# Graph layers on one Trainium2 core: GpSimd's gathers wait for a nearer product

## The chip, the core and the metric

The kernel runs on one core of one Trainium2 chip. The metric is device time in microseconds (us) from start to end of one execution; of several executions the median counts. The engines are TensorE (PE in the profile; its weight loads are PEld), VectorE (DVE), ScalarE (ACT), GpSimd (POOL) and SyncE (SP). They have a queue of instructions each and meet by semaphores.

## What is computed

Four residual blocks on 6250 nodes with 256 features, joined by 106,250 directed edges sorted by target: a graph block, a feed-forward block with 8 experts, a second graph block, a second feed-forward block with 8 experts. Each graph block holds two graph convolutions, so there are four edge sums, called layers 0 to 3 here. The reference, cut to the edge sums:

```python
# first graph block (layers 0 and 1)
deg_out = segment_sum(edge_weight, src); deg_in = segment_sum(edge_weight, dst)
norm = edge_weight * rsqrt(deg_out[src] * deg_in[dst] + EPS)
h6 = relu(segment_sum((h5 @ W6)[src] * norm[:, None], dst) + b6)
h7 = relu(segment_sum((h6 @ W7)[src] * norm[:, None], dst) + b7)
out = h7 @ Wp + bp
# second graph block (layers 2 and 3): the norm comes from target degrees alone
m = (h @ W)[src] * norm[:, None]
x1 = segment_sum(m, dst) + b
...
x = x + gnn0(layernorm(x)); x = x + ffn0(layernorm(x))
x = x + gnn1(layernorm(x)); x = x + ffn1(layernorm(x))
```

## The kernel before

**Tiling.** The edges lie in chunks of 128, and four chunks (`Q`) make a group: 208 groups (`NGR`) in layers 0 and 1. In layers 2 and 3 part of the edge sum is done as products with tables of counts, and 116 groups (`NGK`) are left. The nodes are 49 tiles (`NT`) of 128 rows. For each group GpSimd fetches the rows of the source nodes from a table in HBM, four indirect DMAs (line 915) of 128 rows of about 1 KB, each to the partitions of one chunk. TensorE multiplies these rows by a selection matrix of the group, four chunk products summed in PSUM (line 1091); the product has the sums of the group's edges by target node. VectorE adds it to `ACC`, the sums of all nodes (line 2102).

**The ring of rows.** The gathered rows go to `RS_` = 8 slots of one group each, in layer 0 up to group 37 also to 11 further slots in a tile that is needed for something else later; in layers 2 and 3 a ring of `RK` = 4 slots is used. `gather_edges` is GpSimd's loop over the groups. Ahead of a group's four gathers it waits on the semaphore `s_p`, which counts the products of TensorE, until the product of the group that held the slot before is done: the group eight back in the middle of layers 0 and 1, four back in layers 2 and 3. The first groups of a layer find free slots. `BEGIN` = (0, 208, 416, 532) holds the count of products at a layer's start.

**TensorE**, `sum_edges` (from line 1259): for each group it waits for the group's rows (`wait_rows`, one semaphore per slot, line 1265) and for its scaled selection matrix, makes the product and counts it in `s_p`. In between stand pieces of other work as soon as a tile of nodes has its sums: its transposes (`early_turn`, line 1129), the next layer's dense products (lines 1134 and 1136 in layer 0), and in layers 2 and 3 the products with the counts (lines 1219 and 1239).

**VectorE**, in layer 0 `sum_weighted`, per group g and in this order:

```python
multiply_degrees(g + 3)   # line 2276: waits until the rows of group g+3 have landed
invert(g + 2)             # line 2282, after a square root on ScalarE (line 1562)
...                       # selection for group g+4 (line 2066)
weigh(g + 2)              # line 2286; ScalarE then scales the selection (line 1569)
...                       # degrees and places of group g+4 (lines 2091, 2075)
ve.wait_ge(s_p, g + 1)
step(add_sums(g % 4, spot))   # line 2102, two instructions
```

The out-degree of a source node comes with its row, which is why the weights of layer 0 need the rows. In layers 1 to 3 VectorE makes the selections and the adds, and touches no gathered row; ScalarE scales the selection of layer 1 (line 1639).

The order on each engine is the order of the code; no scheduler moves it.

Of the kernel before, what the change touches and what calls it, by code (L numbers as in the profile page):

```python
# [20 lines left out]
RS_ = 8  # L21
# [4 lines left out]
NC = -(-(-(-NE // P)) // 16) * 16  # L26
NGR = NC // Q
AHEAD = 4
BEHIND = 5
UP, DOWN = 2, 4  # L30
W = 64
# [31 lines left out]
RK = 4  # L63
# [3 lines left out]
BEGIN = (0, NGR, 2 * NGR, 2 * NGR + NGK)  # L67
# [3 lines left out]
def ready_groups(pace, groups):  # L71
    done = [max(0, ((g - pace[1]) * pace[0]) >> 10) for g in range(groups)]
    return [min([g for g in range(groups) if done[g] > t], default=groups) for t in range(NT)]


READY = [ready_groups(pace, groups) for pace, groups in zip(PACE, GROUPS_OF)]
TAIL = min(t for t in range(NT) if READY[0][t] + AHEAD >= NGR)
EARLY = [{READY[layer][t] + AHEAD: t for t in range(TAIL)} for layer in range(3)]
assert all(g + 4 < NGR for g in EARLY[0] if EARLY[0][g] < TAIL - 1)
assert all(g + DOWN < NGR and g + UP + 1 < NGR for g in EARLY[1] if EARLY[1][g] < TAIL - 1)  # L80
assert NT - TAIL == 3 and all(len(early) == TAIL for early in EARLY)
assert all(READY[layer][TAIL - 1] + AHEAD + 2 == GROUPS_OF[layer] for layer in range(3))
KV = Q + 1
# [54 lines left out]
def gnn_ffn(nc, x, src, dst, edge_weight, W6, b6, W7, b7, Wp, bp, Wr, br, W1a, b1a, W2a, b2a, gamma, beta,  # L138
# [23 lines left out]
    with ctx:  # L162
# [3 lines left out]
        def sem(name):  # L166
            return ctx.enter_context(nc.semaphore(name))
# [116 lines left out]
        NS = len(SEL)  # L284
        assert NS > AHEAD
        META = WORK[:, 3 * U * D:3 * U * D + 2 * EC]
# [153 lines left out]
        s_p, s_pe = sem("sums_ready"), sem("sums_more")  # L440
# [49 lines left out]
        def in_x(layer, g):  # L490

            return layer == 0 and g < 2 * ROUND and g % ROUND >= RS_

        def turn_of(layer, g):

            n = BEGIN[layer] + g
            return n % ROUND + n // ROUND * RS_ if n < 2 * ROUND else n - 2 * PX

        def group_of_turn(m):

            return m % RS_ + m // RS_ * ROUND if m < 2 * RS_ else m + 2 * PX
# [3 lines left out]
        def late_turn(layer, g):  # L505
            return divmod(BEGIN[layer] - BEGIN[2] + g, RK)

        def slot_of(layer, g):
            if layer >= 2:
                return late_turn(layer, g)[1]  # L510
            return g % ROUND - RS_ if in_x(layer, g) else turn_of(layer, g) % RS_

        def rows_of(layer, g):
            if layer >= 2:
                return LATE_ROWS[slot_of(layer, g) * Q:(slot_of(layer, g) + 1) * Q]
            return (ROWS_X if in_x(layer, g) else ROWS)[slot_of(layer, g) * Q:(slot_of(layer, g) + 1) * Q]
# [362 lines left out]
        def _(po):  # L879
# [18 lines left out]
            def gather_edges(layer, tab, width):  # L898
                for g in range(GROUPS_OF[layer]):
                    m = turn_of(layer, g)  # L900
                    if layer == 2 and g < RK:
                        po.wait_ge(s_free, 4 + BEGIN[2])
                    elif layer >= 2:
                        po.wait_ge(s_p, BEGIN[layer] + g - RK + 1)
                    elif in_x(layer, g):
                        if g >= ROUND:
                            po.wait_ge(s_p, g - ROUND + 1)
                    elif m >= RS_:
                        po.wait_ge(s_p, group_of_turn(m - RS_) + 1)
                    if layer == 0 and 2 <= g < ROUND:  # L910
                        po.wait_ge(s_dp, RS_ * (g - 1))
                    landed = (s_rx if in_x(layer, g) else s_row)[slot_of(layer, g)]
                    for k, rows in enumerate(rows_of(layer, g)):
                        c = Q * g + k
                        po.indirect_dma_start(  # L915
                            out=rows[:, 0:width], out_offset=None, in_=tab[:, :],
                            in_offset=bass.IndirectOffsetOnAxis(ap=SRC[:, c:c + 1].bitcast(u32), axis=0))\
                            .then_inc(landed, 16)
# [39 lines left out]
            po.wait_ge(s_dost, 16)  # L958
            po.wait_ge(s_span, 1)
            gather_edges(0, tab1, ROW1)  # L960
            gather_wide(tab1, ROW1)

            table_stored(TAB2)
            po.wait_ge(s_sums, 1)
            gather_edges(1, tab2, D)
            gather_wide(tab2, D)
            po.sem_inc(s_wi, 1)

            table_stored(TAB3)
            gather_edges(2, tab3, D)  # L970
            gather_wide(tab3, D)
            table_stored(TAB4)
# [18 lines left out]
            def tokens(n):  # L991
                rows = min(P, CAP - n % RB * P)
                col = n // RB % 2 * RB + n % RB
                return rows, bass.IndirectOffsetOnAxis(ap=IDB[0:rows, col:col + 1].bitcast(u32), axis=0)

            po.wait_ge(s_by, 16 * NI)
            po.wait_ge(s_out, 16 * (NI + 1))
            for n in range(E1 * RB + BEHIND):
                if n < E1 * RB:
                    rows, which = tokens(n)  # L1000
                    po.wait_ge(s_idb, n // RB + 1)
                    if n >= U:
                        po.wait_ge(s_sum, n - U + 1)
                    po.indirect_dma_start(out=XIN[0:rows, n % U * D:(n % U + 1) * D], out_offset=None,
                                          in_=before_y[:, :], in_offset=which).then_inc(s_xg[n % U], 16)
                if n >= BEHIND:
                    m = n - BEHIND
                    rows, which = tokens(m)
# [841 lines left out]
        def _(ve):  # L1850
# [191 lines left out]
            def load_window(g):  # L2042
                if g % RS_ == 0:
                    firsts[g // RS_] = first_nodes(g)
# [10 lines left out]
            def edges(v, g):  # L2055
                return v[:, bass.ds(Q * g, Q)]
# [7 lines left out]
            def select(into, places):  # L2064

                return ve.tensor_tensor(  # L2066
                    by_window(into), PLACES[:, 0:W].rearrange("p (a n) -> p a n", a=1).to_broadcast([P, Q, W]),
                    by_edge(places).to_broadcast([P, Q, W]), ALU.is_equal)
# [15 lines left out]
            def number_places():  # L2084

                step(ve.tensor_copy(PLACES, IOTA[:, :]))
                settle()
# [200 lines left out]
            def sum_weighted():  # L2288

                number_places()  # L2290
                for g in range(AHEAD):
                    load_window(g)
                    load_spots(g)
                    step(place(SEL[g], edges(DST, g)))
                ve.wait_ge(s_sz, 1 + len(SPREADS))
                for g in range(AHEAD):
                    step(select(SELD, edges(REL, g)))
# [1068 lines left out]
```

## Time and profile before

| | us |
|---|---|
| median of 3 runs | 5292.09 (5290.26 to 5301.05) |
| profiled execution, first to last instruction | 5305.9 |
| TensorE busy | 3977.3 (75%) |
| VectorE busy | 2919.9 (55%) |
| GpSimd busy | 2859.7 (54%) |
| GpSimd's gathers of edge rows (line 915) into the ring, 2504 | 2411.9 |
| layer 0, first to last gather | 240.4 to 1533.8 |
| layer 1 | 1558.9 to 2856.3 |
| layer 2 | 3271.8 to 3990.2 |
| layer 3 | 4013.7 to 4707.3 |

The profiled execution's own time is its span; with the profiler it lies 13.8 us above the median. Before layer 0 stand the first normalisation, the first dense product and the degrees; between layers 1 and 2 the first feed-forward block; after layer 3 the second. Busy times are averages over these stages, and no engine is full: in the four edge sums what matters is who waits for whom. A row of the timeline tells an instruction's start, its duration, engine and line, and in brackets how long its engine stood idle before it and what ended that; "remote" is a wait whose end fits no instruction just finished.

### The profile page before, as it was taken

To read this page: it belongs to the slowest core of one execution; us is meant where nothing else is said; L and a number is where in the kernel's file an instruction comes from. 1 tells how busy PE (TensorE), PEld (TensorE's weight loads), DVE (VectorE), ACT (ScalarE), POOL (GpSimd) and SP (SyncE) were. 2 spreads that over 40 slices of the span, in tenths; PEclk is the share of its full clock that TensorE was granted. 3 is DMA by queue.
4 is the path that set the end of the run, shared out by engine and by line. 5 is a ranking of instruction groups with operands and counts; after the bars stand their busy time and mean duration, and the time that the engine had idled before them with its cause. 6 is when DMAs were issued, how large, how long until landed. Compare 5 with 4: busy or idle time off the path is not lost.

```text
span 5305.9 us, 64097 instructions
## 1 busy us (share of the span) xinstructions
PE 3977.3 (75%) x20960; PEld 3151.6 (59%) x20961; DVE 2919.9 (55%) x7680; ACT 1417.2 (27%) x3894; POOL 2859.7 (54%) x3104
## 2 busy tenths in 40 slices
PE   6775655454555576777777996899996898886999
PEld 6653434343434455666666665787785777764666
DVE  7755655455546775555656556776665332243344
ACT  6603323232331222222222331333331000033221
POOL 7745566666656665565653002566565666643322
PEclk9857776777777777777777998999998999997999
DMA  3332343333333232222322002444444554444321
GB/s 92 106 70 78 110 112 100 98 99 99 97 95 90 86 87 79 81 85 81 86 81 66 25 14 74 130 144 144 138 146 140 160 155 138 138 136 135 103 80 54
DMA packets 337524, 535.23 MB, mean 101 GB/s; under 512 B 91587, under 2 KB 246452, under 8 KB 337186
## 3 DMA queue, kind: packets, MB, share of 16 engines
q0 software_dynamic: 133168, 361.15, 24.1%
q1 hardware_dynamic: 196902, 163.10, 10.0%
q10 hardware_dynamic: 7118, 6.83, 0.4%
q8 instruction: 171, 2.80, 0.2%
q14 instruction: 165, 1.35, 0.1%
HBM read 439.58 MB, written 94.26 MB: 101 GB/s over the span
## 4 chain that ended last, share of the span: by engine, by line
PE 54%; DVE 19%; issue 11%; another core or an unknown queue 11%; ACT 2%; DVEq 1%; POOL 1%; DMA 0%; ACTq 0%; SPq 0%; POOLq 0%
PE PSA L1091 15%; PE PSA L1239 12%; PE PSA L1486 4%; PE PSA L1472 4%; PE PSA L1248 4%; DVE ACC L2102 3%; PE PSA L1373 3%; PE PSA L1389 3%; DVE XIN L2075 2%; DVE XT L2075 2%; PE PSA L1041 1%; PE PSA L1219 1%; ACT ACC L1536 1%; DVE PSA L2066 1%
## 5 line engine op out<-in xcount | busy, mean ns | idle before, releaser
L915 POOL DMA_INDIRECT WORK<-tab,SRC x2504 | 2411.9, 963 | 1923.8 <-issue 666.6
L2102 DVE TENSOR_TENSOR ACC<-ACC,PSA 64x256 f32 x1296 | 541.9, 418 | 1221.2 <-remote 686.6
L1091 PE MATMUL PSA<-WORK,XIN 128*128 128x256 f32 x3032 | 881.2, 443 | 362.7 <-ACT XIN L1569 156.8
L1091 PEld LDWEIGHTS PSA<-WORK,XIN 128*128 128x128 f32 x3032 | 653.7, 225 | 490.5 <-issue 387.9
L1091 PE MATMUL PSA<-WORK,XT 128*128 128x256 f32 x1976 | 581.2, 446 | 217.8 <-ACT XT L1569 131.9
L1091 PEld LDWEIGHTS PSA<-WORK,XT 128*128 128x128 f32 x1976 | 427.7, 226 | 302.6 <-issue 226.4
L1239 PE MATMUL PSA<-WORK 128*128 128x256 bf16 x2730 | 367.0, 278 | 16.7 <-issue 16.5
L1239 PEld LDWEIGHTS PSA<-WORK 128*128 128x128 bf16 x2730 | 270.1, 100 | 60.7 <-issue 24.7
L2075 DVE TENSOR_TENSOR XIN<-PSA,DST 128x512 f32<-128x512 f32 x392 | 265.3, 679 | 3.9 <-issue 1.9
L1729 ACT ACTIVATE WORK<-PSA 128x512 bf16<-128x512 f32 x245 | 146.4, 598 | 428.1 <-PE PSA L1219 328.4
L1639 ACT ACTIVATE XIN<-XIN,HSB 128x128 f32<-128x128 f32 x504 | 160.2, 392 | 359.7 <-DVE XIN L2075 231.5
L1248 PE MATMUL PSA<-WORK 128*128 128x50 f32 x832 | 133.6, 313 | 133.1 <-DVE XT L2075 84.8
L1486 PE MATMUL PSA<-ACC,WORK 128*128 128x256 f32 (+1 forms) x1024 | 230.3, 379 | 0.0
L1248 PEld LDWEIGHTS PSA<-WORK 128*128 128x128 f32 x832 | 127.1, 230 | 151.1 <-DVE XT L2075 94.5
L1472 PE MATMUL PSA<-WORK,ACC 128*128 128x489 f32 (+1 forms) x512 | 213.4, 577 | 0.4 <-ACT WORK L1834 0.4
L1248 PE MATMUL PSA<-WORK,XT 128*128 128x50 f32 x832 | 132.5, 312 | 105.5 <-issue 55.6
L1486 PEld LDWEIGHTS PSA<-ACC,WORK 128*128 128x128 f32 (+1 forms) x1024 | 185.7, 185 | 31.4 <-issue 3.5
L1248 PEld LDWEIGHTS PSA<-WORK,XT 128*128 128x128 f32 x832 | 129.1, 231 | 120.9 <-issue 60.6
L954 POOL TENSOR_SCALAR ACC<-IOTA,ACC,HSB 128x64 f32<-128x64 int16 x312 | 177.0, 582 | 36.3 <-PE PSA L1041 19.7
L1041 PE MATMUL PSA<-ACC 128*64 128x98 f32 x1664 | 163.3, 252 | 44.2 <-ACT ACC L1536 43.2
L1802 ACT ACTIVATE WORK<-PSA 128x256 f32<-128x256 f32 x51 | 19.6, 385 | 651.4 <-remote 331.3
L2771 DVE TENSOR_TENSOR WORK<-WORK,PSA 128x10 f32 x208 | 33.6, 162 | 277.0 <-remote 166.0
(511 smaller groups left out, 6768.4 us busy)
## 6 DMA issues: line engine op xcount, KB each, us to landing
WORK<-tab,SRC POOLq DMA_INDIRECT x2504
unit_counts_d<-WORK SPq DMA_DIRECT2D x245, 128.0 KB
WAX<-unit_counts_d SPq DMA_DIRECT2D x140, 128.0 KB
ACC<-in_L_ffn_w SPq DMA_DIRECT2D x16, 1024.0 KB
WORK<-unit_counts_d SPq DMA_DIRECT2D x105, 128.0 KB
tab<-WORK SPq DMA_DIRECT2D x98, 128.0 KB
slots_x<-FILL SPq DMA_DIRECT2D x4, 2080.0 KB
ACC<-slots_x SPq DMA_DIRECT2D x8, 910.0 KB
```

Of the source, the lines that this page charges most:

```text
L915: po.indirect_dma_start(out=rows[:, 0:width], out_offset=None, in_=tab[:, :], in_offset=bass.IndirectOffsetOnAxis(ap=SRC[:, c:c + 1].bitca ...
L954: last = po.tensor_scalar(LOWW[:, k * LOW:(k + 1) * LOW], IOTA[:, 0:LOW], S_LO[:, c:c + 1], EW[:, c:c + 1], ALU.is_equal, ALU.mult)
L1041: last = pe.matmul(hsrc, LOWW[:, k * LOW:(k + 1) * LOW], HI[:, k * HIGH:(k + 1) * HIGH], start=(b == 0 and j == 0), stop=(b == NBT - 1 and ...
L1091: last = pe.matmul(PS[h][:, 0:D], chosen[:, j * P:(j + 1) * P], rows[:, 0:D], start=(j == 0), stop=(j == Q - 1))
L1239: last = pe.matmul(UNS[i][t % 2], UNC[i][n % len(UNC[i])][:, part * P:(part + 1) * P], part_of(2 * u + h, c), start=(u == 0 and h == 0 and ...
L1248: last = pe.matmul(MOVES, TO[k % 2][:, j * P:(j + 1) * P], MOVED[k // Q % 2][:, c * 2 * KX:(c + 1) * 2 * KX], start=(j == 0), stop=(j == Q ...
L1373: last = pe.matmul(PS[q % 4][:, 0:GT // 2], W1S[:, w:w + P], XT0[:, c * GT + hf * (GT // 2):c * GT + (hf + 1) * (GT // 2)], start=(c == 0) ...
L1472: last = pe.matmul(PS[q % 4][:, 0:hn], W1L[:, w:w + P], XT1[:, c * CAP + h0:c * CAP + h0 + hn], start=(c == 0), stop=(c == KC - 1))
L1486: last = pe.matmul(PS[BK + r % BK][0:rows, 0:D], H1[:, f * CAP + r * P:f * CAP + r * P + rows], W2L[:, (k * FC1 + f) * D:(k * FC1 + f + 1) ...
L1639: last = ac.activation(part, part, ACT.Copy, scale=NRM[:, Q * g + j:Q * g + j + 1])
L2075: return ve.tensor_tensor(by_place(into), PLACES.rearrange("p (a n) -> p a n", a=1).to_broadcast([P, Q, P]), by_edge(places).to_broadcast( ...
L2102: return ve.tensor_tensor(rows, rows, PS[h][half, 0:D], ALU.add)
```

## The change

A second wait ahead of a group's gathers, on the same semaphore. In layer 0 from group 60 on, group g waits until the product of group g-4 is counted; in layer 1 from group 8 on, and in layers 2 and 3 from group 4 on, until that of group g-3 is. The old waits stay; except where the slots of the layer's first groups are free, they are met when the new one is. No instruction of an engine is added, taken away or moved besides: the 572 waits (148, 200, 112 and 112) stand on GpSimd's queue, each ahead of the first of a group's four gathers. In the changed file the lines behind the two additions are three further down (915 becomes 918).

```diff
 AHEAD = 4
+NEAR = (4, 3, 3, 3)
 BEHIND = 5
...
                     if layer == 0 and 2 <= g < ROUND:
                         po.wait_ge(s_dp, RS_ * (g - 1))
+                    if g >= (60, RS_, RK, RK)[layer]:
+                        po.wait_ge(s_p, BEGIN[layer] + g - NEAR[layer] + 1)
                     landed = (s_rx if in_x(layer, g) else s_row)[slot_of(layer, g)]
                     for k, rows in enumerate(rows_of(layer, g)):
```

## Rows read from the trace of the kernel before

**Rows 1.** The page: the chain that ended last, shares of the span by engine.
```profile
PE 54%; DVE 19%; issue 11%; another core or an unknown queue 11%; ACT 2%; DVEq 1%; POOL 1%; DMA 0%; ACTq 0%; SPq 0%; POOLq 0%
```
**Rows 2.** Windows, layers 0-3: length, busy us of PE, PEld, DVE, ACT, POOL; clock, DMA, GB/s.
```profile
680.00:1534.00 854.00, 450.79 (x1475) 333.52 (x1474) 448.08 (x1336) 257.75 (x814) 562.79 (x594) 0.72 0.36 98
...
1621.00:2857.00 1236.00, 874.57 (x3989) 749.58 (x3990) 773.95 (x1867) 288.88 (x926) 770.60 (x788) 0.78 0.29 84
3309.00:3990.00 681.00, 624.33 (x4515) 529.20 (x4516) 468.83 (x1113) 225.87 (x507) 417.83 (x436) 0.98 0.47 140
4060.00:4707.00 647.00, 578.43 (x4048) 478.61 (x4046) 203.30 (x456) 18.88 (x49) 410.25 (x431) 0.96 0.50 146
```
**Rows 3.** Lines of 680 to 1534: count, busy us, mean ns, idle before by cause.
```profile
L915 POOL DMA_INDIRECT WORK<-tab,SRC x594 | 562.8, 947 | 291.3 <-issue 170.2 <-remote 104.9 <-PE PSA L1091 16.1
```
**Rows 4.** Waits of 680 to 1534: us in total, times, longest us.
```profile
POOL WORK L915 <- remote: 104.9, 31, 4.0
```
**Rows 5.** Timeline, one burst of layer 0: start, us, engine, line [idle before].
```profile
1012.63 0.95 POOL L915 DMA_INDIRECT WORK<-tab,SRC  x1 [3.90 <-remote]
...
1013.84 0.23 DVE L2276 TENSOR_TENSOR PRD<-DIE,WORK 128x4 f32<-128x4 f32 x1
...
1016.15 3.75 PE L1091 MATMUL PSA<-WORK,XIN 128*128 128x256 f32 x8 [6.05 <-ACT XIN L1569]
...
1021.42 1.89 PE L1091 MATMUL PSA<-WORK,XT 128*128 128x256 f32 x8
...
1026.37 1.97 PE L1091 MATMUL PSA<-WORK,XIN 128*128 128x256 f32 x8 [1.11 <-ACT XIN L1569]
...
1035.50 0.85 DVE L2102 TENSOR_TENSOR ACC<-ACC,PSA 64x256 f32 x2 [9.62 <-remote]
1035.63 0.95 POOL L915 DMA_INDIRECT WORK<-tab,SRC  x1 [3.27 <-remote]
```
**Rows 6.** Timeline, layer 0 while GpSimd issues nothing: two of nine adds, then GpSimd.
```profile
574.71 0.85 DVE L2102 TENSOR_TENSOR ACC<-ACC,PSA 64x256 f32 x2 [3.80 <-PE PSA L1091]
...
601.33 0.85 DVE L2102 TENSOR_TENSOR ACC<-ACC,PSA 64x256 f32 x2
604.02 0.95 POOL L915 DMA_INDIRECT WORK<-tab,SRC  x1 [31.95 <-PE PSA L1091]
```
**Rows 7.** Timeline of GpSimd in the last stage.
```profile
4757.80 0.97 POOL L986 DMA_INDIRECT slots_x<-WORK,IDS  x1 [0.30 <-issue]
```
**Rows 8.** Timeline, the ends of layers 0 and 1: gathers and last adds.
```profile
1532.84 0.95 POOL L915 DMA_INDIRECT WORK<-tab,SRC  x1 [0.30 <-issue]
...
1549.08 0.85 DVE L2102 TENSOR_TENSOR ACC<-ACC,PSA 64x256 f32 x2 [1.10 <-PE PSA L1091]
...
2851.05 0.94 POOL L915 DMA_INDIRECT WORK<-tab,SRC  x1 [2.06 <-PE PSA L1091]
...
2880.01 0.85 DVE L2102 TENSOR_TENSOR ACC<-ACC,PSA 64x256 f32 x2 [2.31 <-PE PSA L1091]
```
**Rows 9.** Timeline, the start of layer 1.
```profile
1558.89 0.95 POOL L915 DMA_INDIRECT WORK<-tab,SRC  x1 [25.10 <-SPq L696]
...
1572.66 0.95 POOL L915 DMA_INDIRECT WORK<-tab,SRC  x1 [0.30 <-issue]
1573.38 0.85 DVE L2102 TENSOR_TENSOR ACC<-ACC,PSA 64x256 f32 x2 [17.93 <-issue]
...
1575.45 1.99 PE L1091 MATMUL PSA<-WORK,XIN 128*128 128x256 f32 x8 [0.56 <-DMA WORK<-tab,SRC]
...
1620.96 0.95 POOL L915 DMA_INDIRECT WORK<-tab,SRC  x1 [5.28 <-remote]
```
**Rows 10.** Timeline, GpSimd in layer 2: first and last gather of one group, then the next.
```profile
3455.05 0.95 POOL L915 DMA_INDIRECT WORK<-tab,SRC  x1 [1.39 <-PE PSA L1091]
...
3458.90 0.95 POOL L915 DMA_INDIRECT WORK<-tab,SRC  x1 [0.30 <-issue]
...
3461.07 0.95 POOL L915 DMA_INDIRECT WORK<-tab,SRC  x1 [1.22 <-PE PSA L1091]
```

## The prediction

> **What bounds the kernel now.** I read the chain of waits first, to learn where the end is decided, then the busy time by stage, then single bursts in the timeline. The chain [rows 1] gives TensorE 54% and VectorE 19%, but also 11% to "another core or an unknown queue", on a kernel with one core: the engine waited for a signal whose sender had, by its own rows, finished long before. Those stretches lie in the four edge-sum stages, so I read these by themselves. In the windows [rows 2] one group (four gathers) takes 854/148.5 = 5.75 us in layer 0, 1236/197 = 6.27 in layer 1, 681/109 = 6.25 in layer 2 and 647/107.75 = 6.00 in layer 3. GpSimd needs 0.947 us for a gather and 0.30 us to the next, 5.0 us per group. In layer 0 that is almost all there is: of the 854 us, 562.8 are busy, 170.2 are those 0.30 us steps, and only 104.9 + 16.1 us are waits for products [rows 3], 31 of them labelled remote [rows 4], 3.4 us each. Layer 0 is bound by GpSimd plus one pause of 3.4 us per four or five groups. In layers 1 to 3 GpSimd's four gathers cost 5.0 us of 6.0 to 6.3, so it waits after every one to three groups: the ring is full and each gather is let go by a product. There the summing side is the bound.
>
> How the two sides meet is in the timeline of layer 0 [rows 5]. GpSimd starts at 1012.63 and issues 16 gathers without a stop, to 1032.36. The product at 1021.42 ends by its row at 1023.31, the third one after it starts at 1026.37 and ends at 1028.34, yet VectorE gets the first of these signals only for its add at 1035.50, after 9.62 us idle, and GpSimd resumes at 1035.63, 3.27 us after its own last gather. While GpSimd is idle, from 572.07 to 604.02, nothing like it occurs: nine adds from 574.71 to 601.33, 3.33 us per group [rows 6]. So while gathers are issued without a break, TensorE's signals can come late, and a pause of GpSimd lets them through.
>
> *The Trainium skill's page "Perfetto Trace Analysis", section "Tensor Engine Instruction (MATMUL, LD_WEIGHTS)", says that a matmul's end in a trace is estimated from its size, and that its signal goes out only when PSUM has acknowledged the data. By it the product may in truth have ended late, and the row at 1021.42 alone can't refute that; the idle stretch [rows 6] speaks for GpSimd as the cause either way.*
>
> **The change part by part.** No instruction moves on any engine. A group's first gather waits in addition for a nearer product: four back in layer 0 from group 60 on, three back elsewhere, where it was eight back (layers 0 and 1) or four back (layers 2 and 3). Queued behind that wait on GpSimd are only the following gathers; who then waits for these is VectorE in layer 0 (line 2276 needs the rows of group g+3 before the add of group g) and TensorE in layers 1 to 3. There are 148 + 200 + 112 + 112 = 572 such waits.
>
> 1. *The waits themselves.* Every one is a further wait ahead of a gather that has one already. The nearest row is the gather at 4757.80 in the last stage: its code has two waits too, both met, and its distance to the one before is the usual 0.30 us [rows 7]. So I take 0; the row's last digit allows 0.02 us, 572 x 0.02 = 11 us at most.
>
> 2. *Layer 0, the switch at group 60.* GpSimd must wait there for a product that lies four groups later. At 3.33 us per group with GpSimd idle [rows 6] that is 13.3 us in place of one ordinary pause of 3.4: its queue is 10 us later. At the layer's end it gets some back: now the last gather ends at 1533.79 and the last add at 1549.93, 16.1 us later [rows 8]. With four groups left, the last rows must land, 1.84 us (a gather ends at 1573.61 and the product that waits for it starts at 1575.45 [rows 9]), and pass multiply, weights and product. I take 12 us, between 8.8 (landing, the 6.1 us chain of step 3, one add of 0.85) and the 16.1 of today: 4 us back. Sum +6, bounds -4 (if the summing side, not GpSimd's queue, sets the end) and +10.
>
> 3. *Layer 0, steady.* After a pause three products are signalled together, so three groups may go, 15.0 us. The fourth needs the next product. Its weights come after VectorE's multiply for the first group gathered since the pause: that lands at 4.7 + 1.84 = 6.6 us. From a multiply at 1013.84 to the end of the product that it leads to, 1016.15 + 3.75 = 1019.90, it is 6.1 us [rows 5]. So the permission comes at 12.7 us, 2.3 us before it is wanted, bursts stay at four, and the term is 0. Without that slack bursts get shorter: two groups cost (10.0 + 2.06)/2 = 6.03 us per group (2.06 is the pause after two groups at 2851.05 [rows 8]), so +0.28 x 148 = +41 us; one group 5.0 + 1.3 = 6.3 [rows 10], +81 us; three lie near +20 us, an estimate between zero and 41.
>
> 4. *Layer 1, the switch at group 8.* Now GpSimd issues eleven groups in one go to 1615.68 and resumes at 1620.96, and from the first add at 1573.38 on only four adds fall into that time [rows 9]. With the change it stops after eight, 1558.89 + 8 x 5.0 = 1599. From there I give four groups 3.33 us each: six adds by 1612 instead of four by 1621, that is 9 + 2 x 6.27 = 21 us ahead. At the end the last eight groups take 2880.01 - 2851.05 = 29 us, 3.6 each [rows 8], because no gather runs beside most of them; with three left, five of them go at 6.27, +13 us. Sum -8, bounds -21 and +13.
>
> 5. *Layers 1 to 3, steady.* GpSimd is let go by products before and after: in layer 2 it starts at 3455.05, its last gather starts at 3458.90, the next group starts at 3461.07 behind a product's signal after 1.22 us [rows 10]. The same signal lets go a group that is nearer by one (layers 2, 3) or five (layer 1); GpSimd's starts don't move. The rows must then be there in time: a group lands 4.7 + 1.84 = 6.6 us after the signal, and three groups at 6.0 to 6.3 us leave 18 us. Term 0; the one group of difference at start and end of layers 2 and 3 is (6.25 - 3.33) = 2.9 us won and about the same lost, +-3 each.
>
> Sum: +6 + 0 - 8 + 0 + 0 = -2 us. The profiled execution has a span of 5305.9 us, 13.8 above the median of 5292.09; the terms are differences and I put them on the median: 5290 us. The outer bounds of the five terms, without a change of burst length, give -31 to +40; all extremes together are unlikely, and half of it, 5276 to 5312, holds most of this case.
>
> **The rivals.** *Slower: layer 0 loses its lead.* VectorE takes its work in order, and the multiply of group g+3 stands ahead of the add of group g. Four deep, every landing lies just ahead of that multiply: the 2.3 us of slack in step 3 is hardly more than the difference between a product that takes 3.75 us and one that takes 1.89 [rows 5]. It decides from the point at which the product four back comes later than 15 us into a burst. Bursts of two to three groups give +20 to +41, 5310 to 5333.
>
> *The Trainium skill's "DMA: Bandwidth & Descriptors", section "Rules for kernel authors", advises to issue a DMA early and to wait for it late, so that its fixed cost lies beside other work. The change issues 572 groups later than the ring allows; by that rule it ends on this rival's side. The rows bear that out for layer 0 only, where the slack is small; in layers 1 to 3 step 5 shows 18 us to cover 6.6.*
>
> *Faster: less run-ahead, shorter stalls.* If the late signals [rows 5] come from long unbroken bursts, a GpSimd that runs out of permissions sooner lets them through sooner. For it speaks the start of layer 1 [rows 9], where the burst of eleven groups stops the adds; against it that in the steady stages the ring is full and permissions are used as they come, so that the bursts are set by the products and not by the depth, and that layer 0 can't go below GpSimd's own 5.0 us. If half of layer 0's 121 us of pauses went, 5232; if layer 1 went from 6.27 to 6.03 us per group, -47 us, 5245. I put it at 5240.
>
> *The wait never bites* (the product three or four back is always signalled already): then nothing moves, 5292. Against it stands that GpSimd is seen waiting for the product eight back.
>
> **How the numbers follow.** Forecast of terms 1 to 5: chance 0.38, at 5290. Slower rival: 0.28. Faster rival: 0.26. No effect: 0.08. Bounds of 0.2% (10.6 us, about what can be told from no change): the forecast's own spread gives 0.30 within, 0.05 below and 0.03 above. So faster 0.26 + 0.05 = 0.31, same 0.30 + 0.08 = 0.38, slower 0.28 + 0.03 = 0.31. Both signs hold a good part, so the range goes from the middle of the faster rival to the two-group end of the slower one: 5240 to 5335; the likeliest case's own range is 5276 to 5312.
>
> **What would show it.** Right: in layer 0 GpSimd still pauses once in four or five groups for some 3.4 us, with one longer pause of about 13 us at group 60 and adds that follow each other by 3.3 us in it; in layer 1 GpSimd stops after eight groups, near 1599; layers 2 and 3 keep 6.0 to 6.3 us per group; gathers behind a met wait stay 0.30 us apart. Wrong: VectorE's multiply (line 2276, three lines further down) with long waits for a DMA, and bursts of one to two groups, would show the slower rival; layer 1 or 2 well below 6 us per group, and less remote waiting in front of the adds, the faster one; gathers over 0.32 us apart behind the waits would charge step 1.

## The result: 1.9% slower, most of it in layer 2

The changed kernel takes 5397.36 us in the median of 3 runs (5392.79 to 5401.16) against 5292.09 before: a ratio of 1.0192 with a 95% interval of 1.0174 to 1.021, 105 us. The profiled execution has a span of 5395.4 us against 5305.9. The chain of the page, which answers to [rows 1], covers only 72% of the span now and names no culprit:

```profile
PE 44%; DVE 9%; issue 8%; another core or an unknown queue 7%; POOL 2%; DVEq 1%; ACT 1%; DMA 0%; SPq 0%; POOLq 0%; ACTq 0%
```

The stages do. From a layer's first add to its last one (starts of line 2102, which is 2105 now):

| us | layer 0 | layer 1 | layer 2 | layer 3 |
|---|---|---|---|---|
| before | 1129.4 | 1306.6 | 717.1 | 689.7 |
| changed | 1141.1 | 1309.5 | 792.2 | 694.3 |
| difference | +11.7 | +2.9 | +75.1 | +4.6 |

What lies outside the four stages is 5 us shorter (the differences add up to 94.3 us, the whole execution to 89.5). How far such a number moves by itself can be seen in the profiles of the experiments below where the layer was untouched: 1121 to 1134 us for layer 0, 1300 to 1328 for layer 1, 717 to 725 for layer 2, 679 to 690 for layer 3. So only layer 2 stands far out of the noise of one profile; layer 0 lies 7 us and layer 3 some 5 us above their ranges. One profile may overstate its share: by the medians of the experiments below, the change in layer 2 alone costs 1.05% and in the other three layers 0.71%.

The windows of layers 0 and 2 answer to [rows 2]; columns as there:

```profile
680.00:1543.00 863.00, 521.71 (x1479) 362.09 (x1478) 447.36 (x1340) 253.38 (x815) 559.12 (x592) 0.73 0.35 97
3317.00:4080.00 763.00, 659.16 (x4562) 550.30 (x4563) 473.19 (x1117) 225.92 (x512) 415.58 (x438) 0.95 0.42 126
```

Layer 0 keeps its pace, 863/148 = 5.83 us per group after 5.75; layer 2 falls from 6.25 to 763/109.5 = 6.97, with GpSimd as busy as before. What it waits for there, before and changed, is in the waits of layer 2 (us in total, times, longest):

```profile
POOL WORK L915 <- PE PSA L1091: 91.4, 55, 7.8
ACT WORK L1729 <- remote: 79.6, 25, 5.8
POOL WORK L915 <- remote: 70.2, 52, 3.0
DVE WORK L2366 <- remote: 26.6, 20, 3.1
```
```profile
ACT WORK L1732 <- remote: 202.8, 45, 6.5
POOL WORK L918 <- PE PSA L1094: 181.8, 67, 9.5
DVE WORK L2369 <- remote: 120.9, 39, 5.6
POOL WORK L918 <- remote: 50.2, 21, 2.7
```

GpSimd waits for products 70 us longer. That alone would be what less lead looks like, but TensorE never waits for gathered rows in this window (7.0 us in two waits just before it). Instead ScalarE's copies (line 1732) and VectorE's selections (line 2369), the two partners of TensorE in the count products (line 1222) that run between the groups, wait two and a half times and four and a half times as long for remote signals, those whose sender had long finished by its own rows.

The timeline shows both things that differ. First a single start, before (the add belongs to the gather at 3461.07 in [rows 10]) and changed: VectorE's add and GpSimd's first gather are let go by the same product's signal.

```profile
3461.01 0.85 DVE L2102 TENSOR_TENSOR ACC<-ACC,PSA 64x256 f32 x2 [1.99 <-PE PSA L1091]
```
```profile
3478.43 0.85 DVE L2105 TENSOR_TENSOR ACC<-ACC,PSA 64x256 f32 x2 [2.40 <-PE PSA L1094]
...
3478.96 0.94 POOL L918 DMA_INDIRECT WORK<-tab,SRC  x1 [1.74 <-PE PSA L1094]
...
3480.60 1.89 PE L1094 MATMUL PSA<-WORK,XIN 128*128 128x256 f32 x8
...
3483.97 0.95 POOL L918 DMA_INDIRECT WORK<-tab,SRC  x1 [0.30 <-issue]
...
3490.49 0.60 ACT L1732 ACTIVATE WORK<-PSA 128x512 bf16<-128x512 f32 x1 [5.17 <-remote]
...
3491.23 0.38 PE L1222 MATMUL PSA<-WORK 128*128 128x256 bf16 x2 [4.08 <-ACT WORK L1732]
...
3493.79 2.52 PE L1094 MATMUL PSA<-WORK,XT 128*128 128x256 f32 x8
...
3497.07 0.94 POOL L918 DMA_INDIRECT WORK<-tab,SRC  x1 [8.40 <-PE PSA L1094]
```

Before, GpSimd starts 0.06 us after the add; now 0.53 us. Taken from the signal itself, the median over the layer's pauses is 0.26 us before and 0.74 us now: **a resumed GpSimd comes 0.48 us later** (in layers 1 and 3 the medians are 0.26 and 0.76). Second, it then issues two groups without a stop (3483.97 follows after 0.30 us), ScalarE gets no signal until 3490.49, TensorE has nothing to do, and the next product starts only at 3493.79. Before, 104 of 107 bursts in this layer were one group long; now 52 are one group and 28 are two.

TensorE's granted clock falls behind such a stall. It is 1.00 (2.4 GHz) from 3484 to 3491, where TensorE stands idle at the end, and 0.72, a mean of its levels of 1.2 and 2.4 GHz, in the six microseconds that follow; the product at 3493.79 takes 2.52 us, the one at 3480.60 took 1.89:

```profile
3491.00:3497.00 6.00, 5.77 (x30) 4.68 (x31) 2.31 (x6) 1.79 (x5) 0.00 (x0) 0.72 0.19 66
```

Over the windows of layer 2 the clock is 0.95 after 0.98 before, and TensorE is busy 35 us longer for 47 more matmuls.

### The profile page after: what moved, and what is told of

Read it like the earlier page. It is cut to its first block, busy times and chain, and to the rows that moved or that the text cites. A ratio compares the mean times of both kernels' runs of the same rounds, so it can differ in the third digit from the quotient of the medians.

```text
span 5395.4 us, 64669 instructions
## 1 busy us (share of the span) xinstructions
PE 4086.3 (76%) x20960; PEld 3201.7 (59%) x20961; DVE 2923.7 (54%) x7680; ACT 1406.9 (26%) x3894; POOL 2848.8 (53%) x3104
## 4 chain that ended last, share of the span: by engine, by line
PE 44%; DVE 9%; issue 8%; another core or an unknown queue 7%; POOL 2%; DVEq 1%; ACT 1%; DMA 0%; SPq 0%; POOLq 0%; ACTq 0%
PE PSA L1094 11%; PE PSA L1242 10%; PE PSA L1489 4%; PE PSA L1475 4%; PE PSA L1392 3%; PE PSA L1376 3%; PE PSA L1251 3%; PE PSA L1222 1%; DVE ACC L2105 1%; DVE XT L2078 1%; POOL WORK L918 1%; PE PSA L1139 1%; POOL slots_x L989 1%; DVE XIN L2078 1%
## 5 line engine op out<-in xcount | busy, mean ns | idle before, releaser
L1094 PE MATMUL PSA<-WORK,XIN 128*128 128x256 f32 x3032 | 937.2, 463 | 328.9 <-ACT XIN L1572 131.9
L1094 PEld LDWEIGHTS PSA<-WORK,XIN 128*128 128x128 f32 x3032 | 682.0, 235 | 490.6 <-issue 364.0
L1094 PE MATMUL PSA<-WORK,XT 128*128 128x256 f32 x1976 | 602.7, 458 | 190.4 <-ACT XT L1572 95.9
L2279 DVE TENSOR_TENSOR PRD<-DIE,WORK 128x4 f32<-128x4 f32 x186 | 31.1, 168 | 372.4 <-DMA WORK<-tab,SRC 366.5
L1565 ACT ACTIVATE DRT<-PRD,EPSD 128x4 f32<-128x4 f32 x208 | 61.6, 297 | 638.7 <-DVE PRD L2279 323.6
```

Source lines behind the costliest of these rows:

```text
L1094: last = pe.matmul(PS[h][:, 0:D], chosen[:, j * P:(j + 1) * P], rows[:, 0:D], start=(j == 0), stop=(j == Q - 1))
```

## The experiments

Two theories were set against each other. **A**: the cost is the wait as an instruction. A gather holds one wait itself. A second one becomes an instruction of its own on GpSimd's queue, ahead of the gather; the built program has 667 such instructions on GpSimd instead of 95. Which wait goes where follows from the order in the code: the one written first stays with the gather, and in the change that is the old one, long met, while the new one, which binds, is the separate instruction. **B**: the cost is the nearer product, that is less lead. Every ratio is against the kernel before on the same chip. Its median there is given beside the time; where it isn't, it was 5295.25 us, and 5294.09 for the bursts of two.

**The second wait without a nearer product.**

```diff
-NEAR = (4, 3, 3, 3)
+NEAR = (8, 8, 4, 4)
```

> The second wait stays, as an instruction of its own on GpSimd's queue ahead of a group's first gather, but it asks for nothing nearer: eight back in layers 0 and 1, four back in layers 2 and 3, as the old one. Theory A (the separate wait instruction lets GpSimd resume some 0.5 us after the signal where the gather's own wait resumes after 0.26, and this disturbs the lockstep of layer 2): layer 2 is again some 75 us longer, the whole 5370 to 5400. Theory B (the nearer product, less lead): nothing changes, 5285 to 5300.

Measured: 5389.38 us, ratio 1.0141 (1.009 to 1.0192). Layer 2 took 794.4 us, with 28 bursts of two. Its starts, in the timeline:

```profile
3610.66 0.85 DVE L2105 TENSOR_TENSOR ACC<-ACC,PSA 64x256 f32 x2 [2.27 <-remote]
3611.20 0.94 POOL L918 DMA_INDIRECT WORK<-tab,SRC  x1 [1.70 <-remote]
```

0.54 us again, as theory A said. The whole loss of layer 2 is there with no nearer product asked for. Of the whole kernel's 1.92% this run has 1.41%; its four runs lie up to 44 us apart, and the two intervals overlap.

**The nearer product without a second wait.** The new wait takes the place of the old one.

```diff
+                    if g >= (60, RS_, RK, RK)[layer]:
+                        po.wait_ge(s_p, BEGIN[layer] + g - NEAR[layer] + 1)
-                    if layer == 2 and g < RK:
+                    elif layer == 2 and g < RK:
                         po.wait_ge(s_free, 4 + BEGIN[2])
...
-                    if g >= (60, RS_, RK, RK)[layer]:
-                        po.wait_ge(s_p, BEGIN[layer] + g - NEAR[layer] + 1)
```

> The nearer wait takes the place of the old one, so each group's first gather carries it itself and no instruction is added. Depths as in the change (four back in layer 0 from group 60, three back elsewhere). Theory A (the wait instruction): GpSimd resumes 0.26 us after a signal again and the time returns to 5275 to 5300. Theory B (less lead): 5380 to 5400 as with the change, layer 2 again about 75 us longer.

Measured: 5280.77 us, ratio 0.9958 (0.9936 to 0.9981), faster than the kernel before; layer 2 took 715.7 us. GpSimd's queue has 95 wait instructions again. Theory B has fallen, with its sign, for leads of three and four groups.

**Both waits, in the other order.** The lines of the new wait stand ahead of the old one's.

```diff
                     m = turn_of(layer, g)
+                    if g >= (60, RS_, RK, RK)[layer]:
+                        po.wait_ge(s_p, BEGIN[layer] + g - NEAR[layer] + 1)
                     if layer == 2 and g < RK:
...
-                    if g >= (60, RS_, RK, RK)[layer]:
-                        po.wait_ge(s_p, BEGIN[layer] + g - NEAR[layer] + 1)
```

> Both waits as in the change, written in the other order: now the gather itself carries the nearer wait, the one that binds, and the separate wait instruction ahead of it asks for the older product, which is long done. As many instructions and the same depths as in the change. Theory A1 (the instruction costs only where it is the one that is waited for): like the single wait, 5270 to 5295, GpSimd resumes 0.26 us after the signal. Theory A2 (any further instruction ahead of a gather costs): 5350 to 5400.

Measured: 5291.99 us beside 5312.49 of the kernel before on that chip, ratio 0.9964 (0.9946 to 0.9982); layer 2 took 708.7 us.

```profile
3613.26 0.85 DVE L2105 TENSOR_TENSOR ACC<-ACC,PSA 64x256 f32 x2 [1.78 <-PE PSA L1094]
3613.32 0.94 POOL L918 DMA_INDIRECT WORK<-tab,SRC  x1 [1.39 <-PE PSA L1094]
```

The start is back at 0.06 us with the same 667 instructions. So the instruction costs nothing that shows when it is met, and 0.48 us when it is what GpSimd waits for. In layer 0, which GpSimd bounds, a group's first gather inside a burst follows after 0.30 us with the instruction as without. Two lines in another order are worth 2.3% (1.0192 against 0.9964).

**Two wait instructions in layer 2.** The kernel before, and ahead of each gather group of layer 2 four more waits for the same product, which the build packs in two instructions.

```diff
+NEAR = (8, 8, 4, 4)
...
+                    for again in range(4 if layer == 2 and g >= RK else 0):
+                        po.wait_ge(s_p, BEGIN[layer] + g - NEAR[layer] + 1)
```

> The kernel before, with two separate wait instructions ahead of each group in layer 2 alone, both asking for the same product as the old wait, four back. If each instruction that is waited on adds its own half microsecond: GpSimd resumes 1.2 us after the signal and layer 2 is 110 to 150 us longer than before (717). If the second one passes unseen: 0.75 us and some 75 us longer, as with one. If the loss is only a matter of where the resumed burst falls: less than 60 us longer.

Measured: 5402.68 us beside 5312.49, ratio 1.017 (1.0147 to 1.0193). GpSimd resumes 0.85 us after the signal in the median, against 0.74 with one instruction and 0.26 with none: the second adds 0.11 us, not another half. Layer 2 took 804.3 us, 87 more than before, nearest to the second of the three expectations.

**Layer 2 alone, and all but layer 2.** The condition of the change is narrowed.

```diff
-                    if g >= (60, RS_, RK, RK)[layer]:
+                    if layer == 2 and g >= RK:
```
```diff
-                    if g >= (60, RS_, RK, RK)[layer]:
+                    if layer != 2 and g >= (60, RS_, RK, RK)[layer]:
```

> The change in layer 2 alone. If the stages add up, layer 2 is 70 to 80 us longer and the whole 5365 to 5375; both theories say so. If what layers 0 and 1 hand on sets layer 2's rhythm, it is below 5330.

> The change in layers 0, 1 and 3, not in layer 2. If the stages add up: layer 0 +12, layer 1 +3, layer 3 +5, layer 2 as before, the whole 5305 to 5325. If layer 2 is upset by what comes before it: above 5360.

Measured: 5356.82 us, ratio 1.0105 (1.0069 to 1.0142), layer 2 at 792.7; and 5334.97 us, ratio 1.0071 (1.0048 to 1.0094), layer 2 at 724.5. The parts add up, 1.05% and 0.71% to 1.76%, within the interval of the whole change. The first lies 8 us under what was expected, the second 10 us above: layers 0, 1 and 3 pay 0.7%, which the single profile of the changed kernel shows only in part (+11.7, +2.9 and +4.6 us). Some 190 pauses in these layers at 0.48 us would be 91 us; 38 were measured. That part of the delay falls where GpSimd is ahead would explain it, but is not shown.

**Bursts of two without a late start.** 81 pauses at 0.48 us are 39 us; layer 2 lost 75. Six of the other 36 stand in its rows: in groups 26, 52, 78 and 104 GpSimd stands idle for 2.04 us ahead of the second gather, where it was 0.54 before. The changed kernel, then the kernel before, group 26:

```profile
3461.59 1.10 POOL L918 DMA_INDIRECT WORK<-tab,SRC  x1 [2.04 <-issue]
```
```profile
3433.05 1.12 POOL L915 DMA_INDIRECT WORK<-tab,SRC  x1 [0.54 <-issue]
```

In layer 1 six groups have the like (1.69 us, at most 0.36 before). It comes only in the layers and runs where the separate instruction ends GpSimd's pauses, and not with the waits in the other order or with the single one; its cause is open. Are the bursts of two the rest? In the kernel before, layer 2 alone:

```diff
+                    elif layer == 2 and g < NGK - 1:
+                        if not g % 2:
+                            po.wait_ge(s_p, BEGIN[layer] + g - RK + 2)
                     elif layer >= 2:
                         po.wait_ge(s_p, BEGIN[layer] + g - RK + 1)
```

> The kernel before, but in layer 2 GpSimd waits once for two groups, for the later of their two products, and then issues both without a stop: bursts of two everywhere, no separate wait instruction, GpSimd resumes 0.26 us after the signal. Theory C (of the 75 us that layer 2 lost, the part over 81 pauses x 0.48 = 39 us comes from bursts of two, during which TensorE's signals to ScalarE and VectorE come late): layer 2 is 30 us and more longer than before (717). Theory D (bursts of two are harmless, all of the loss is the later resuming): layer 2 stays at 705 to 725.

Measured: 5483.81 us, ratio 1.0357 (1.033 to 1.0384). Layer 2 took 916.2 us, 199 more than before, 8.0 us per group, with starts 0.26 us after the signal. From its waits and its timeline in layer 2:

```profile
ACT WORK L1732 <- remote: 361.8, 74, 8.2
POOL WORK L918 <- PE PSA L1094: 344.3, 54, 9.6
```
```profile
3608.71 0.95 POOL L918 DMA_INDIRECT WORK<-tab,SRC  x1 [6.32 <-PE PSA L1094]
...
3612.98 0.60 ACT L1732 ACTIVATE WORK<-PSA 128x512 bf16<-128x512 f32 x1 [1.30 <-PE PSA L1222]
...
3617.47 0.94 POOL L918 DMA_INDIRECT WORK<-tab,SRC  x1 [0.30 <-issue]
3620.18 0.60 ACT L1732 ACTIVATE WORK<-PSA 128x512 bf16<-128x512 f32 x1 [5.60 <-remote]
```

The burst runs from 3608.71 to 3618.41. ScalarE does a copy at 3612.98 and two short instructions, then stands idle for 5.60 us until 1.8 us after the burst: the relay between TensorE and ScalarE, some two rounds per group, stands still in the later part of a long burst. TensorE waits for no gathered rows in this layer, so it isn't lead that is short. 53 bursts of two cost 199 us, 3.8 us each. At that price the 28 of the changed kernel would cost 105 us, more than the 30 left to be explained; the pairs also wait for the later of two products, so the price per burst can't be carried over. That bursts of two harm layer 2 is shown; that they make up exactly the rest is not. Some of the rest is TensorE's lower clock behind the stalls (0.95 in the changed kernel, 0.91 here), which these runs don't separate.

**How much lead is enough, and where the gain comes from.** All with the single wait: two back in layers 1 to 3; only layers 2 and 3; only layers 0 and 1; and the whole once more.

```diff
-NEAR = (4, 3, 3, 3)
+NEAR = (4, 2, 2, 2)
```
```diff
-                    if g >= (60, RS_, RK, RK)[layer]:
+                    if layer >= 2 and g >= RK:
```
```diff
-                    if g >= (60, RS_, RK, RK)[layer]:
+                    if layer < 2 and g >= (60, RS_)[layer]:
```

> One wait, carried by the gather, two back in layers 1 to 3 and four back in layer 0. Tests the lead by itself: rows land 6.6 us after the signal, two groups at 6.0 to 6.3 us leave 12. If lead is not short: 5265 to 5300, as with three back. If it is: layers 1 to 3 lose 1 us and more per group, 5400 and more, with waits of the products for a DMA.

> One wait, carried by the gather, three back in layers 2 and 3 only; layers 0 and 1 as before. If the 0.4% of the single-wait kernel come from layer 3 (676 against 690 us in the profiles): 5275 to 5285. If they come from the starts and steady stages of layers 0 and 1: 5290 to 5300.

> One wait, carried by the gather, in layers 0 (four back from group 60) and 1 (three back from group 8) only; layers 2 and 3 as before. If the 0.4% of the single-wait kernel are half from here (layers 2 and 3 alone gave 0.2%): a ratio of 0.997 to 0.999. If layers 0 and 1 give nothing: 0.999 to 1.001.

> The single-wait kernel (four back in layer 0 from group 60, three back elsewhere) once more with more rounds. If its gain is real: a ratio of 0.994 to 0.998 again. If the first measurement was luck, layers 0 and 1 alone having given nothing: 0.998 to 1.001.

| single wait | median, us | before, same chip | ratio (95%) | layer 2, us |
|---|---|---|---|---|
| four / two / two / two back | 5311.68 | 5312.49 | 1.0004 (0.9988 to 1.002) | 714.6 |
| layers 2 and 3, three back | 5302.35 | 5312.49 | 0.9977 (0.9959 to 0.9995) | 703.4 |
| layers 0 and 1, four and three back | 5295.67 | 5294.09 | 1.0 (0.9985 to 1.0015) | 724.4 |
| all, again | 5295.2 | 5319.18 | 0.9957 (0.9941 to 0.9972) | 706.8 |

The expected times were set from 5292 us; where the kernel before takes 5312, the ratio is what can be compared. Two back, the whole is as long as before, but the 0.4% that three back gains are gone, and lead begins to be short: in layer 1 (1600 to 2900 us) TensorE's waits for gathered rows, three back and then two back, are

```profile
PE PSA L1094 <- DMA WORK<-tab,SRC: 14.9, 5, 4.8
```
```profile
PE PSA L1094 <- DMA WORK<-tab,SRC: 94.0, 51, 5.3
```

and the kernel before has none there. The whole single-wait kernel beats the kernel before by 0.42 and 0.43%; its lead over the one with layers 2 and 3 alone is within the intervals. Layer 2 carries some of that: 703 to 716 us in the five profiles in which the gather itself carries a nearer wait there, 717 to 725 in the three with the old one. The parts measured apart give 0.23% and 0.0% against 0.43% for the whole. The intervals leave room for that, and why a nearer product helps layer 2 wasn't found.

## Why the prediction was wrong

It forecast 5290 us in a range of 5240 to 5335; 5397 lies outside. It called the sum of its five terms -2 us; the change cost 105. The side of the slower rival came true, not its mechanism, and that is luck.

**Step 1 failed: the waits.** It took 572 waits at 0 because the gather of [rows 7], with two waits in its code, follows its neighbour after 0.30 us. That row has a wait that was met in advance, and for those the zero holds: it is what the other order of the two waits gave. But step 5 says of the same waits that GpSimd is let go by them, group after group. A wait that ends a pause had to be priced at a pause. The trace of before has one such row among the gathers of rows, the one that opens layer 0; its separate instruction waits for a store (line 739), and it starts 0.89 us after that store's last recorded signal, where layer 1's first gather, which is let go by its own wait, starts after 0.26:

```profile
240.41 1.21 POOL L915 DMA_INDIRECT WORK<-tab,SRC  x1 [18.67 <-DMA tab<-HSB]
```

The bound of 11 us was drawn from the last digit of the wrong row. Measured: 0.48 us per resume, 0.11 for a second instruction. The sign that was to charge this step, gathers over 0.32 us apart, was set for waits that are met; 109 groups of layer 0 still follow after 0.30 us, and the cost stands in the pauses.

*The Trainium skill's "Perfetto Trace Analysis", section "Identifying Dependency Chains", says that an instruction with waits on several engines may get EventSemaphore instructions ahead of it for the further conditions. That is what the build did here, for two waits on one semaphore; where such an instruction ended a pause in layer 2, GpSimd resumed 0.48 us later.*

**Step 2, the switch in layer 0,** gave +6. The pause is there, though shorter than the 13.3 us put down for it, and it is followed by the first ordinary one (GpSimd's starts after the two pauses):

```profile
683.21 0.94 POOL L918 DMA_INDIRECT WORK<-tab,SRC  x1 [8.24 <-PE PSA L1094]
...
706.43 0.94 POOL L918 DMA_INDIRECT WORK<-tab,SRC  x1 [3.52 <-PE PSA L1094]
```

The layer's +11.7 us hold 37 later resumes too; with the single wait, which has the same switch, it took 1126.4 and 1130.9 us, as before, so the +6 can't be seen.

**Step 3, layer 0 steady, was right.** Bursts stay at four (35 of 37), one pause of 3.5 us each. What was feared as the slower rival did come, VectorE's multiply now waits for rows, and costs nothing, because it replaces the wait of the adds; these are the lines of layer 0, first GpSimd's, which answers to [rows 3], then the adds (337.2 us idle before them in the kernel before, 289.8 of it remote), then the multiply (7.5 before):

```profile
L918 POOL DMA_INDIRECT WORK<-tab,SRC x592 | 559.5, 945 | 308.9 <-issue 169.2 <-PE PSA L1094 88.1 <-remote 51.6
...
L2105 DVE TENSOR_TENSOR ACC<-ACC,PSA 64x256 f32 x298 | 124.8, 419 | 7.3 <-issue 0.7
...
L2279 DVE TENSOR_TENSOR PRD<-DIE,WORK 128x4 f32<-128x4 f32 x148 | 24.6, 166 | 365.4 <-DMA WORK<-tab,SRC 360.6 <-issue 4.7
```

GpSimd bounds this layer in both kernels, and VectorE waits some 340 to 370 us either way. It also weakens the reading of [rows 5] as signals held up by an unbroken burst: bursts are as long as before here, and the adds wait 7 us in all. (The product at 1026.37 there is the second after the one at 1021.42, not the third; nothing hangs on it.)

**Step 4, the start of layer 1,** went as described: GpSimd stops after eight groups and resumes after 11.97 us, and VectorE does its sixth add before that:

```profile
1564.43 0.94 POOL L918 DMA_INDIRECT WORK<-tab,SRC  x1 [21.03 <-SPq L697]
1618.09 0.94 POOL L918 DMA_INDIRECT WORK<-tab,SRC  x1 [11.97 <-PE PSA L1094]
```
```profile
1617.53 0.85 DVE L2105 TENSOR_TENSOR ACC<-ACC,PSA 64x256 f32 x2 [3.30 <-PE PSA L1094]
```

That is 53 us after the layer's first gather for six adds; before, it was 62 us for four. The -8 us forecast for the layer can't be told from its spread; the single wait in layers 0 and 1 alone moved the time by 0.0%, so the earlier adds brought no gain that shows.

**Step 5 was right on lead and wrong on the starts.** 18 us to cover 6.6 is enough, as the single-wait kernel shows (15 us of waits for rows in layer 1); two groups would have been tight. But "GpSimd's starts don't move" fell with step 1, and in layer 2 the rhythm broke with them: one group per product before, many bursts of two after. In the burst above the next product ends before the burst is over (3480.60 + 1.89 = 3482.49, ahead of 3483.97), so GpSimd runs on. But a group that starts 0.74 us after its signal leaves GpSimd free 5.7 us after it, and before, 95 of 110 groups in this layer started 6.0 to 6.25 us after the one ahead; the later start alone doesn't close that distance, and what breaks the rhythm stays open. Layer 3, already mostly in bursts of two before (40 of 67), cost 5 us in this profile; it took 694 to 700 us in the three profiles with the separate instruction and 679 to 690 where it was untouched.

**The rule on early issue did not decide.** *The Trainium skill's page "DMA: Bandwidth & Descriptors", section "Rules for kernel authors", advises to issue a DMA early and wait late. With the single wait the gathers are issued later than the ring allows, and the time is 0.4% shorter.* With two groups of lead the gain is gone and TensorE waits for rows in layer 1 (94 us), so the lead can't be cut much further.

## What to carry to other kernels

Ask of every wait whether it will be met on arrival or will end a pause: the first may be free, the second can cost a later start at each pause, on the path of whoever waits behind it. Where one instruction needs two conditions on one semaphore, wait only for the later one; where it needs two semaphores, write the one that binds so that the instruction itself carries it (tried here with one semaphore only), and look in the built program where each has gone. In a loop of engines that let each other go, half a microsecond can cost more than itself, so price a stage by its rhythm and not only by counting.

## What the runs showed of the hardware

In layers 1 to 3 GpSimd's gather starts 0.26 us after the signal that it carries as its own wait (medians). Where a separate wait instruction stands for the signal, it starts after 0.74 us in layer 2 and 0.76 in layers 1 and 3, and after 0.85 us where two stand ahead of it in layer 2. A separate wait that is met before the gather's turn costs nothing that these runs can tell. Where separate waits end the pauses, the second gather of a few groups starts up to 2.0 us after the first has ended, instead of 0.4 to 0.5. While GpSimd issues eight gathers without a stop, ScalarE's waits for TensorE in layer 2 grow (361.8 us remote against 79.6); through what the two meet stays open.
